# Convolution by image, channel third and half: 130-row patch columns, three bank pairs, and each third of the matrices fetched when its products end

## The reference, cut to what matters

```python
x = _L0_conv_ref(x, ...)   # window attention on 8x8 windows, then an MLP (48 -> 192 -> 48), both with residuals
x = _L1_conv_ref(x, ...)   # inverted bottleneck, below

h = jnp.einsum('oc,bchw->bohw', w1, x)             # expand 48 -> 288 channels
h = jax.nn.relu(_bn(h, g1, b1, m1, v1))
h = jax.lax.conv_general_dilated(h, wd, (1, 1), ((1, 1), (1, 1)), feature_group_count=HID, ...)  # 3x3 depthwise
h = jax.nn.relu(_bn(h, gd, bd, md, vd))
h = jnp.einsum('oc,bchw->bohw', w2, h)             # project 288 -> 48
return x + _bn(h, g2, b2, m2, v2)
```

## Time and profile before

| What | Value |
|---|---|
| median of 3 runs | 1933.91 us (1924.66 to 1934.29) |
| profiled execution, and its span | 1929.11 us, 1927.3 us |
| PE busy | 1783.9 us, 93% of the span |
| DVE busy | 1446.4 us, 75% |
| ACT busy | 1091.0 us, 57% |
| POOL busy | 418.4 us, 22% |
| mean granted clock | 0.974 |

### The profile page before, as it was taken

How to read it: one execution, slowest core, us unless ns; L and a number is a source line. 1 busy time by engine, 2 the same in 40 slices (tenths; PEclk the granted TensorE clock), 3 DMA queues, 4 the chain that set the end, 5 groups by cost and what they waited for, 6 DMA issues and landing times.

```text
span 1927.3 us, 75807 instructions
## 1 busy us (share of the span) xinstructions
PE 1783.9 (93%) x30728; PEld 1410.8 (73%) x30728; DVE 1446.4 (75%) x2570; ACT 1091.0 (57%) x2550; POOL 418.4 (22%) x804
## 2 busy tenths in 40 slices
PE   5999999999999998799999888998988898999987
PEld 4888888888888886455555777777767777877765
DVE  4999999999999998566667566565656566666655
ACT  2888888888888886455555533343434343434432
POOL 4333333333333332502200440010101010101000
PEclk9999999999999999799999999899999999999989
DMA  1222222222222221677765566635545445545441
GB/s 66 70 73 78 73 78 74 76 74 77 74 77 75 76 76 63 164 185 175 169 151 139 154 149 160 139 80 128 125 110 124 115 98 136 112 112 132 101 119 39
DMA packets 286893, 206.94 MB, mean 107 GB/s; under 512 B 225927, under 2 KB 275560, under 8 KB 276840
## 3 DMA queue, kind: packets, MB, share of 16 engines
q1 hardware_dynamic: 282562, 197.37, 40.1%
q0 software_dynamic: 2400, 6.42, 1.6%
q10 hardware_dynamic: 1750, 0.39, 0.1%
HBM read 128.54 MB, written 62.98 MB: 99 GB/s over the span
## 4 chain that ended last, share of the span: by engine, by line
PE 48%; DMA 4%; issue 4%; ACT 3%; DVE 0%; SPq 0%; POOL 0%; DVEq 0%; ACTq 0%
PE psum L1183 14%; PE psum L1161 14%; PE psum L1219 6%; PE psum L684 5%; PE psum L665 3%; PE psum L655 3%; ACT h L896 3%; DMA piece<-img_mid 2%; PE psum L670 2%; DMA mats<-in_taps 1%; DMA room<-tok_mid 1%; DMA scaled_taps<-mats 1%; DMA room<-in_ident 0%; ACT room L754 0%; DVE yc L1306 0%
## 5 line engine op out<-in xcount | busy, mean ns | idle before, releaser
L1161 PE MATMUL psum<-ew,xp 64*100 64x96 f32 x6144 | 333.4, 259 | 41.6 <-ACT h L896 20.8
L1161 PEld LDWEIGHTS psum<-ew,xp 64*100 64x100 f32 x6144 | 306.3, 171 | 81.9 <-issue 39.6
L896 ACT ACTIVATE h<-psum 100x384 f32<-100x384 f32 x456 | 208.5, 490 | 255.9 <-PE psum L1161 255.9
L1183 PEld LDWEIGHTS psum<-h,mats 101*64 101x64 f32 x9216 | 287.8, 144 | 67.0 <-issue 66.6
L1183 PE MATMUL psum<-h,mats 101*64 101x64 f32 x9216 | 293.6, 228 | 45.8 <-issue 45.1
L896 ACT ACTIVATE room<-psum 128x512 f32<-128x512 f32 x216 | 129.0, 597 | 245.5 <-PE psum L1183 245.5
L897 DVE TENSOR_SCALAR h<-psum 100x384 f32<-100x384 f32 x312 | 173.4, 556 | 114.6 <-PE psum L1161 103.6
L348 PE MATMUL psum<-kb,qa 128*64 128x256 f32 x2048 | 243.7, 380 | 0.8 <-DVE prob L447 0.8
L935 POOL COPY xp<-piece 128x400 f32<-128x400 f32 x128 | 67.6, 528 | 651.9 <-DMA piece<-img_mid 651.6
L348 PEld LDWEIGHTS psum<-kb,qa 128*64 128x64 f32 x2048 | 140.6, 137 | 56.0 <-issue 1.5
L1284 DVE STREAM_TRANSPOSE room<-room 128x1024 f32<-128x1024 f32 x144 | 173.2, 1229 | 7.9 <-DVE room L897 0.5
(11 more groups left out here) (150 smaller groups left out, 2812.3 us busy)
## 6 DMA issues: line engine op xcount, KB each, us to landing
mats<-scaled_taps SPq DMA_DIRECT2D x63, 896.0 KB, 6.8
tok_mid<-mid SPq DMA_DIRECT2D x128, 224.0 KB, 1.9
room<-tok_mid SPq DMA_DIRECT2D x64, 448.0 KB, 4.4
piece<-img_mid SPq DMA_DIRECT2D x196, 63.8 KB, 2.4
img_mid<-room SPq DMA_DIRECT2D x128, 97.5 KB, 3.2
kb<-kk SPq DMA_DIRECT2D x512, 24.0 KB
scratch<-in_x_tokens SPq DMA_DIRECT2D x126, 96.0 KB, 2.0
out<-yc SPq DMA_DIRECT2D x14, 768.0 KB, 8.6
```

Of the source, the lines that this page charges most:

```text
L896: return nc.scalar.activation(dst, src, ACT.Relu)
L1161: mm = nc.tensor.matmul(ring[(2 * J + u) % 4][0:PIN, p:4 * CH:4], xp[hx][rows, 4 * J + p, :], w1[rows, c, :], start=True, stop=True)
L1183: mm = nc.tensor.matmul(psum[POUT * u:POUT * u + POUT, BANK_OF[d] + n // 8, at:at + 4 * (PATCHES // 2) - n % 4:4], mats[ch // TCH][0:PIN + ...
```

## The change

The chunks now go in the order image, third, half, and both halves of an image have a tile `xp` of their own: chunk k is `place(k)`. So two chunks in a row use the same matrices, and they are loaded in every second chunk (`load_mats`, m counts the loads), tile by tile as its products in the second of the two chunks end. POOL scales all three sets of matrices one after the other, ahead of the pieces of images 1 to 3.

`img_mid` becomes four column strips of 34 columns, neighbours overlapping by two, so that a piece (16 rows now) is contiguous for each channel. DVE writes the overlapping columns in the MLP with four small additions for each strip. `xp` holds columns of patches, 130 rows by 10, so that patches above each other share rows; POOL zeroes it and writes its ones once, and no borders are closed later. Pieces go through two slots, and POOL cuts each with two copies of 48 partitions. Pieces of the next image are loaded in the last third of the current one.

The expand ring has three bank pairs, banks 0 to 5. Since banks 4 and 5 are also project's, group 10 waits for the first two additions of project step 0, and project waits for groups 5 and 13 to be emptied. The output tile `y` exists twice, and a half's output is stored in four DMAs of 384 KB, each of which SP waits for. The residual of the first third is one addition of 512 pixels where there were two of 256.

```diff
-        y = [sb(f"y{s}", [P, WS, GW + 2]) for s in range(2)]
+        y = [sb(f"y{s}", [P, 2, WS, GW // 2 + 2]) for s in range(2)]
...
+                        sp.dma_start(d["img_strips"][:, 2 * k:2 * k + 2, j - 1, :],
+                                     y[1 - s][64 * k:64 * k + C, :, :, :].rearrange("q g r x -> q g (r x)"))\
...
+                    for to, c, column, lanes, of, at, x in ((slice(0, P), 0, end, slice(0, P), 1, 0, 0),
+                                                            (slice(0, P), 1, 0, slice(0, P), 0, n, WS - 1),
+                                                            (low, 1, end, high, 0, 0, 0),
+                                                            (high, 0, 0, low, 1, n, WS - 1)):
+                        nc.vector.tensor_tensor(y[1 - s][to, c, :, column], sums[of][lanes, at, :, x], held[of][lanes, at, :, x],
+                                                ALU.add)
...
+        piece = [sb(f"piece{s}", [P, ROWS, SIDE]) for s in range(2)]
+        xp = [sb(f"xp{s}", [P, PC // 2, H + 2, PW + 2]) for s in range(2)]
...
-        ring = [psum[:, s, :] for s in range(4)]
+        ring = [psum[:, s, :] for s in range(6)]
...
+        def place(k):
+            image, at = divmod(k, 2 * CHUNKS)
+            return image, at // 2, at % 2
...
-                        ring[(2 * J + u) % 4][0:PIN, 0:4 * CH].rearrange("q (c p) -> q c p", p=4))
+                        ring[2 * (J % 8 % 3) + u][0:PIN, 0:4 * CH].rearrange("q (c p) -> q c p", p=4))
...
+        def load_piece(eng, image, hx, j):
+            i = PIECES * (2 * image + hx) + j
+            wait(eng, cut, 2 * (i - 1))
...
+        def cut_piece(pool, image, hx, j):
...
+            for r in range(2):
+                lanes = slice(ONE * r, ONE * r + C)
+                nc.gpsimd.tensor_copy(xp[hx][lanes, :, 1 + ROWS * j:1 + ROWS * (j + 1), :], src[lanes]).then_inc(cut, 1)
+                pool.wait_ge(cut, 2 * i + r + 1)
...
+            def store(image, hx, n):
+                k = 2 * CHUNKS * (image + 1) - 2 + hx
+                sp.wait_ge(y_done, added(k, n, GROUPS4 - 1))
                 for r in range(2):
...
+                    sp.wait_ge(y_stored[hx], 16 * (4 * image + 2 * n + r + 1))
...
+            def load_mats(k):
+                m = k // 2 + 1
+                source = d["taps"] if m < CHUNKS else d["scaled_taps"]
+                for s in range(LOADS):
+                    sp.wait_ge(unit_ready, ready_filter(k, DEPTHS // LOADS * (s + 1) - 1, DPARTS - 1))
...
+            def chunk(k, last):
+                image, c, hx = place(k)
+                if hx == 0 and k < 2 * CHUNKS:
+                    keep_mats(c)
+                if c == CHUNKS - 1 and image + 1 < B:
+                    sp.wait_ge(unit_ready, ready_expand(k, PAIRS_E - 1, 1))
+                    wait(sp, y_done, added(k - 1, NSTEP - 1, GROUPS4 - 1))
+                    for j in range(PIECES):
+                        load_piece(sp, image + 1, hx, j)
+                if not last and hx:
+                    load_mats(k)
+                for n in range(NSTEP):
+                    if hx and c == CHUNKS - 1:
+                        store(image, 0, n)
+                    elif image and hx == c == 0:
+                        store(image - 1, 1, n)
...
-                if J >= 2:
+                if J in (8, 9):
                     pe.wait_ge(*expands_done(k, J - 2, u))
+                elif J == 10 and k:
+                    if u == 0:
+                        pe.wait_ge(y_done, added(k - 1, 0, 1))
...
+                elif J >= 3:
+                    pe.wait_ge(*expands_done(k, J - 3, u))
...
+                if c == 0 and J == 0:
+                    pe.wait_ge(cut, 2 * PIECES * (2 * image + hx + 1))
...
+                    if not last:
+                        for u in range(2):
+                            pe.wait_ge(*expands_done(k + 1, 8 * n + 5, u))
...
+                    if n == g == 0:
+                        wait(dve, y_stored[hx], 64 * image)
```

More of the change, by code:

```diff
@@ new lines, in _ @@
+            assert len(constants) == CONSTANTS
+            constants += [(t[...], 0.0) for t in xp]
+            for hx in range(2):
+                for r in range(2):
+                    lanes = slice(ONE * r + 32, ONE * r + 64)
+                    constants.append((xp[hx][lanes, :, 1:H + 1, :], 1.0))
+                    if hx == r:
+                        edge = (PC // 2 - 1, PW + 1) if hx else (0, 0)
+                        constants.append((xp[hx][lanes, edge[0], 1:H + 1, edge[1]], 0.0))
@@ L979, in _, with put @@
+            assert len(constants) == FIXED
+            def put(first, last):
+                for n in range(first, last):
+                    t, value = constants[n]
+                    nc.gpsimd.memset(t, value).then_inc(fixed, 1)
+                    pool.wait_ge(fixed, n + 1)
+            put(0, CONSTANTS)
             loads = [(ident[:, :], d["ident"]), (w1[0:C, :, :], d["w1T"]), (w1[ONE:ONE + C, :, :], d["w1T"])]
@@ L1133, in chunk @@
                 if last:
                     for n in range(NSTEP):
-                        store_step(k // CHUNKS, n)
-                elif c == CHUNKS - 1:
-                    store(k // CHUNKS)
+                        store(image, 1, n)
             schedule(sp, lambda: None, chunk)
-            sp.wait_ge(y_stored, 32 * HALVES + 32 * NSTEP)
+            for hx in range(2):
+                sp.wait_ge(y_stored[hx], 64 * B)
         @block.tensor
@@ L1192, in first, with chunk @@
                 pe.wait_ge(mlp_done, STRIPS)
-                pe.wait_ge(border_set, 2)
+                pe.wait_ge(fixed, FIXED)
                 for J in range(PAIRS_E):
-                    expand(0, 0, 0, J)
+                    expand(0, J)
                 depthwise(0, 0)
-            def chunk(b, hx, c, last):
-                k = number(b, hx, c)
+            def chunk(k, last):
+                c = place(k)[1]
                 for u in range(1, DEPTHS):
                     depthwise(k, u)
-                if not last and c == CHUNKS - 1:
-                    pe.wait_ge(border_set, 2 * (2 * b + hx + 2))
                 def project(n):
@@ L1285, in turn, with add @@
                                     turned_patches(h2[:, :, BLK * e:BLK * (e + 1)], half)).then_inc(turned, 1)
-            def add(n, g, b, hx, c, k, last):
+            def add(k, n, g, last):
+                image, c, hx = place(k)
                 if g == 0:
```

251 lines of the change are left out of this document (83 added, 168 removed).

## The result

The changed kernel takes 1804.5 us (median of 4 runs, 1801.2 to 1809.7) where the kernel before, on the same chip, takes 1929.3 (1920.8 to 1934.3): a ratio of 0.936, 95% interval 0.931 to 0.941. A second measurement of the same kernel gave 1805.7 us and 0.939 (0.937 to 0.942). The execution profiled here took 1809.7 us, its span is 1807.9, and what follows is told of it.

The account below looks back on a forecast made before the run. PE was taken to bound the kernel, busy 93% of the span, with 93.3 us lost in the convolution. DMA load -57, bank pairs -15, tail +8: -64 us on 1929.1 gives 1865, stated as 1866; range 1838 to 1906.

Parts of the forecast that it names:

- Three bank pairs: Expand in the convolution: a third pair covers PE's waits for ACT; 15 us gain, bounds 0 and 20.8.
- the three waits: Expand of a good chunk: PE waits for ACT at groups 2, 10 and 12, 0.34 + 0.34 + 0.31 us.
- The new wait of group 10: Expand: group 10 waits for two additions by DVE, about 0.1 us, 23 times.
- The DMA load: Convolution: fewer matrix loads and smaller stores cut PE's 93.3 us loss to 36; 57 us gain, bounds 0 and 93.
- Rival 2: Convolution: stops go as the number of matrix sets, 11 / 23 of the loss stay, 45 us; 1877 us, chance 17%.
- Rival 1: Convolution: PE's stops don't come from the DMA load, only pairs and tail count; 1924 us, chance 7%.
- the first rule weighed in the prediction: PE's instruction fetch: refilling 16 KiB blocks is mostly hidden, so stops would have another cause; sum 1922 us.
- The tail: End of the program: SP waits for each of the last four stores, 17.2 us; costs 8 us, bounds 0 and 14.
- The MLP: MLP strips: DVE's four small additions, 0.4 us, fit in 1.25 us of cover before PE's next L665; costs nothing.
- Rival 3: MLP: DVE becomes the bound if small additions cost what full ones do; 17 us more, 1883 us, chance 5%.
- The pieces: Image changes: eight pieces load and are cut in 17 us, matrices fit by 4 us; cost 0, 18 in range.
- Rival 4: Image changes: pieces hold up the matrices, so the kernel gets slower, up to 168 us, 2034 us; chance 7%.

Follow-up runs that it names:

- small stores: Kernel before, with each of its seven stores of a half within the loop writing one channel of 48: 1872.3 us, ratio 0.975.
- 20 sets: Changed kernel, with matrices loaded in every chunk from chunk 6 on, 20 sets instead of 11, the same ones again: 1829.4 us, ratio 0.954.
- small matrices: Kernel before, with loads of matrices from the fourth set on bringing one row of 112: 1878.4 us, ratio 0.978.

## Why the prediction was right and wrong

**Three bank pairs: the step that failed.** The text said that the three waits "have a group more, 0.85 us (5.09 us for 96 records is 6 groups)" and took 15 us, with 20.8 as the upper end. The 0.85 was read as PE's own pace from a row in which PE is busy throughout. It is the round trip of two pairs; PE's pace is 0.74. The term of 15 us measured 58.6 us in the trace, 53 to 61 between the changed kernel with two pairs and with three, and 35 in the kernel before. The upper bound was no bound: I had limited the gain by the idle time that the records show, and most of this wait stands in busy time. That some of the three waits "only lets the array drain" and so stays is shown by no run: with three pairs no wait of expand for ACT is left. In the grouped rows of chunks 0 to 22 expand has, for the same 5888 records, these busy and idle times: before, in the changed kernel with two pairs, and in the changed kernel.

```profile
L1161 PE MATMUL psum<-ew,xp 64*100 64x96 f32 x5888 | 320.1, 259 | 39.3 <-ACT h L896 19.9 <-issue 17.3 <-POOL xp L952 0.4
```

```profile
L1135 PE MATMUL psum<-ew,xp 64*100 64x96 f32 x5888 | 307.8, 253 | 24.1 <-ACT h L894 22.4 <-issue 0.4
```

```profile
L1142 PE MATMUL psum<-ew,xp 64*100 64x96 f32 x5888 | 275.2, 250 | 0.0
```

The last two differ by the pairs alone: 22.4 us of the gain are idle for ACT and 32.6 are busy time, 55 in all. The other 12 us of busy time that the first line has went with the rest of the change, without a third pair. The mean of one record hides the wait (253 and 250 ns, as records overlap). The new wait of group 10 for two additions, priced at 0.1 us, stands in no idle entry; the second eight groups take 0.1 us more (6.00 against 5.89). This term alone put the time below the range.

One rule of the Trainium skill bears on this. "Perfetto Trace Analysis", section "Matmuls", says that independent groups of matmuls should rotate through PSUM banks so that emptying one overlaps the next one's matmuls. The kernel before did that with two pairs, and lost 1.2 us in eight groups; that rule names no number of banks, and of the two and three pairs tried here three left no wait.

**The DMA load: right in its cause, too small in its price.** 57 us forecast, 71 measured; 36 were to stay, 22 did. The shape is as forecast: the first three chunks lose 2 instead of 12, and most of what is left, 14.5 us, lies in the three chunks where stores and several tiles go, which had been priced at 16 with their own sets. Too high was the price of 1.8 for a set that travels alone: in the seven other chunks that load one (3, 7, 9, 13, 15, 19, 21) 5.3 us are lost, 0.8 each. In chunks 3, 9 and 21 no time is lost to it (28.8 us each), although blocks execute while it travels. What makes a block late in one such chunk and not in another is open, and it isn't the program alone: in the second measured execution of the same kernel chunk 9, with its loads issued at the same places, takes 32.9 us with a stop of 2.2.

Which change brought the 71 us was priced by sets, and the stores count for more. An estimate from two traces: with small stores the kernel before loses 41.7 us, 51.6 less than with all bytes, and with 20 sets the changed kernel loses 40.8. So some 50 of the 71 go with the stores of 768 KB that stood ahead of the matrices, and some 20 with the sets that are no longer loaded.

Rival 2, 45 us left, is refuted by the 22, and stops going by the number of sets also by the small matrices: the seven chunks after a store still lose 4.6 us each without a set. Rival 1 is refuted by the small stores and small matrices. The granted clock went to 0.99, as said. Whether a block waits for one packet or for all that is queued, which the prediction weighs, no run shows.

Here the first rule weighed in the prediction is settled for this kernel. By the rows, PE stood 62.4 us on issue before and 14.3 after, always beside stores or matrices, and not at all in chunks that have neither. "Runtime: NRT & Kernel Launch", section "Instruction fetch mechanics", in the Trainium skill, calls the cost of crossing a block mostly hidden: the trace agrees for the chunks without large transfers and not for those with them.

**The tail: right.** 8 us forecast; four stores one by one take 17.1 us to the end, as the 17.2 forecast, and cost 7.4. The other 1.6 of the 9.0 lie in the last project, which ran 7.05 us where it took 5.41, at a granted clock of 0.79 (1783 to 1791 us) against 1.00.

**The MLP: right.** Three lines of one strip, DVE and PE in order of time, for the earlier trace rows:

```profile
906.04 0.61 DVE L732 TENSOR_TENSOR room<-psum,room 128x8 f32<-128x8 f32 x4
...
906.67 0.76 DVE L736 TENSOR_TENSOR room<-psum,room 128x256 f32<-128x256 f32 x2
...
908.06 0.73 PEld L665 LDWEIGHTS psum<-room 128*64 128x64 f32 x8 [0.18 <-ACT room L762]
```

The four small additions take 0.61 us where 0.4 was estimated, and end inside the cover of 1.25: PE's next step waits for ACT. Rival 3 falls.

**The pieces: right.** SP around the change of image, in order of time:

```profile
1209.46 45.39 SPq L945 DMA_DIRECT2D piece<-img_mid  x32
1254.95 1.32 SPq L1086 DMA_DIRECT2D mats<-scaled_taps  x3
1256.32 38.70 SPq L1068 DMA_DIRECT2D out<-yc  x8
```

Eight pieces take 19.4 us in the first half and 19.2 in the second where 17 were forecast (a copy is 732 ns, not 850, and a load 2.4 us), the matrices are issued 20 us into chunk 5 as forecast, the first lands at 1261.6, and PE wants it at 1263.4. That is 1.8 us of room, not 4. No wait for `mats`, `cut` or the stored tile appears in chunks 0 to 22. Rival 4 falls, but not by much.

The forecast of "most chunks 30.5 to 32 us" was wrong in the same step as the sum: fourteen of the 23 take 28.6 to 28.8.

## What to carry to other kernels

Busy time of PE is not its own pace: before a duration is used as the price of work, look at when the engine behind it is released, and whether the intervals are equal; where they are uneven (0.75 and 0.95 us here), look for a wait inside the busy time. Here a deeper ring gave back more than all idle time shown. A stop on issue that comes in chunks with large transfers and not in others is likely a cost of those transfers, and making them small shows it. Here fewer of them, and stores that no longer stood in one row with matrices, helped, while moving them about mostly moved the stop. One stop is no measure: the same place gave 5.87 and 2.10 us, so sums over many chunks are what to compare. And a gain can only be bounded by idle time where the records would show the idle time.

## What the runs showed of the hardware

- PE's records of back-to-back matmuls on small tiles (64x96) hide most of a wait for a bank: eight groups took 6.47 us without an idle entry, and 7.1 with one of 0.34, for work that takes 5.89.
- PE stops on issue beside loads or stores of 384 to 896 KB: over the seven chunks after a store 58.2 and 52.7 us are lost with both kinds, 32.0 with stores alone and 11.2 with matrices alone. A single stop varies by execution: 5.87 and 2.10 us in the same place beside the same stores and matrices.
- After such a stop of 2.60 us the granted clock was 0.50 (1445.7 to 1448.7 us of the changed kernel), and the 320 records behind it took 1.55 us more than at the pace of 11.42 for 384. With small stores it was 0.51 behind the stop of 1.75 us, with small matrices 1.00 behind the one of 1.47 (61 records in 3.46 and 1.97 us).
- 106,000 packets of 136 bytes next to these cost next to nothing (ratio 1.000, 0.996 to 1.005).
- An addition of 128x8 from PSUM takes DVE 0.15 us; a copy of 48x640 takes POOL 0.73 us, where one of 128x400 takes 0.53.
